# Cross-attention and FFN on one core: two more units take their probabilities through VectorE and memory

## The chip, the cores and the metric

The kernel runs on one core of a Trainium2 chip. The metric is the device time of one execution in microseconds; the median of three runs is given. Engines: TensorE (PE; its weight loads are PEld), VectorE (DVE), ScalarE (ACT), GpSimd (POOL), and SyncE (SP), whose queue issues nearly all DMAs, in the order in which they are written and each behind its own waits.

## The reference

```python
x = x + xattn(layernorm(x), ctx, mask, position_bias, ln_weight, w_q, w_k, w_v, w_out)
x = x + ffn(layernorm(x), ...)          # routed scales, sign(weight), bias

def xattn(hidden, kv, attention_mask, position_bias, ...):   # B=8, 128 x 128 tokens, D=512, H=32 heads of 128
    h_q, h_k, h_v = rmsnorm(hidden) @ w_q.T, kv @ w_k.T, kv @ w_v.T
    score = einsum('bqhd,bkhd->bhqk', h_q, h_k) + position_bias
    score = softmax(where(mask, score, -inf))
    score = where(mask, score, 0.0)
    attn = einsum('bhqk,bkhd->bqhd', score, h_v)
    return hidden + attn @ w_out.T
```

## The kernel before

**Stages.** Keys and values of all heads are computed first (to about 310 us of the span) and kept in memory. Then the queries of one pair of heads after another are computed, and between their matmuls the attention of earlier pairs and the output product run. The last stage, from about 755 us, is the FFN. Each large product is made of three matmuls in split precision (a high and a low part of each operand), and each group of 512 x 512 is made of seven such products, so that a group `n` has products 1 to 7, read by ScalarE or VectorE into `ring`.

**A unit** `j` is one head for four of the eight batches (`UNITS`, 64 of them; `j % 2` picks its buffers). Its steps are: `S` scores on TensorE (four 128 x 128 matmuls in two passes), `SC` bias added and row maximum on VectorE, `EXP` four exponentials on ScalarE, `N` scaling by the row sums on VectorE, a transposition, `PV` the context sums on TensorE (probabilities times values), `OH` and `OL` their high and low part on ScalarE and VectorE.

**Two ways to transpose.** A unit that is not in `BLOCKED` takes `T` and `PT`: TensorE transposes four 128 x 128 blocks into the PSUM bank `t` (line 1559), ScalarE copies the bank to `probs_t` (line 1038). A unit in `BLOCKED` takes `TZ`, `TS` and `TL`: ScalarE has written its exponentials to the bank `t` (`exps_of`), VectorE scales them there (line 1302) and transposes 32 x 32 blocks into `probs` (line 1307, `turn_probs`); SyncE issues four stores to `p_turned` in memory (line 762, `probs_store`), waits for them, and loads the blocks at their places to `probs_t` (line 768, `probs_load`). `PV` of such a unit waits for that load. Before, units 0 to 3 and 56 to 63 take the first way and units 4 to 55 the second.

**The order of the work is written out by hand** in `schedule()`: one list of steps, and each engine (SyncE's queue too) walks through those that are its own, in that order. There is no reordering: an instruction that waits holds all behind it on its engine. The units 0 to 3 stand in the branch `p == 0`; from unit 4 on, `aside(j, ...)` writes one unit: `PV` of `j - 2`, `S` and `EXP` of `j + 1`, load of the turned `j`, `normal(j + 1)`, and other work between. In the branch `p == 0` the groups are `first` = 33 and `n` = 34; `load` is the load of the query weights for the group after (`WL`, line 686), `sums` POOL's sums of them (`WS`, lines 855 to 860) and the first split (`WX`, on ScalarE line 971, on POOL line 867); `WOL` is the load of output weights (line 805), `BL` of a position bias (line 798), `KL` of keys (line 781).

**Semaphores that matter.** `d_pstore` and `d_pload` (one for each parity) count stores and loads of turned probabilities; `probs_load(j)` waits for the four stores of `j` and for `PV` of `j - 2`; `scores(j)` waits until `probs` of `j - 2` has been stored or transposed; `exponentials(j)` into the bank `t` wait until that of `j - 1` has been turned or copied.

Of the kernel before, what the change touches and what calls it, by code (L numbers as in the profile page):

```python
# [71 lines left out]
SPLIT = NH - 4  # L72
# [3 lines left out]

BLOCKED = range(4, 2 * SPLIT)


def bias_of(j):
# [9 lines left out]
def parts_of(step):  # L92
    kind, *index = step
    parts = PARTS_OF.get(kind, (kind,))

    if kind == "OUT" and index[0] == LAST - 1:
        parts = parts[:1]
    return [(part, *index) for part in parts]


def schedule():
# [93 lines left out]
    def product(n, i):  # L195
        return [("P", n, i), (READ[i], n)] + ([("SAVE", n, READ[i])] if n < NKV and READ[i] in RESULT else [])
# [47 lines left out]
    def biased(j):  # L244
        found = [("BM", j + 2)]
        if bias_of(j + 2) != bias_of(j + 3):
            found += [("BL", bias_of(j + 2) + 2)]
        return found

    def aside(j, early, middle, late, read_behind=()):  # L250
        found = [("PV", j - 2)] if j - 2 in BLOCKED else [("PV", 3)] if j == 4 else []
        found += [*read_behind, ("S", j + 1), ("EXP", j + 1), *biased(j)]
        return [*found, *early, ("TL", j), *normal(j + 1), *middle, *late]

    def last_aside(j, n, middle):

        six_five, c22 = product(n, 5), product(n, 7)
        found = [("PVH", j - 2), ("S", j + 1), ("EXP", j + 1), *biased(j), *six_five, ("OL", j - 2), *c22]
        if j == 7:

            found = [("PVH", j - 2), ("SP", j + 1), *six_five, ("SC", j + 1), ("EXP", j + 1), *biased(j), ("OL", j - 2), *c22]
        return [*found, ("TL", j), *normal(j + 1), *middle]

    def normal(j):
        return [("N", j), ("TZ", j), ("TS", j)] if j in BLOCKED else [("N", j)]

# [3 lines left out]
    def outs(p, *which):  # L270
        return [("OUT", p, b) for b in which]

    q = at[QUERIES[0]]
    for p in range(SPLIT // 2):
        j = 4 * p
        n = q + p + 2
        prod = {i: product(n, i) for i in SLOT}
        m = NPAIR + p + 2
        load, sums = [], []
        if n + 1 < len(GROUPS):  # L280
            load = [("WL", m + 1, 0), ("WL", m + 1, 1)]
            sums = [("WS", m + 1), ("WX", m + 1, 0)]
        if p == 0:

            first = q + 1
            steps += [*product(first, 7), *prod[1], ("N", 1), ("WX", m, 2), ("PV", 0), ("SMALL",)]
            steps += [("S", 2), *product(first, 3), ("T", 1), ("EXP", 2), ("BM", 3), ("BL", 3), *prod[6], ("N", 2), ("PV", 1)]
            steps += [("S", 3), *product(first, 4), *prod[2], ("WX", m, 3), ("T", 2), ("EXP", 3), ("BM", 4), *prod[5], ("N", 3),
                      ("PV", 2), ("WOL", 1), *load]
            steps += [*prod[7], ("S", 4), *prod[3], ("T", 3), ("EXP", 4), ("BM", 5), ("BL", 4), *prod[4],  # L290
                      *outs(0, 0), *normal(4), ("KL", 2), *sums, *outs(0, 1)]
            continue
        o = p - 1
        final = 2 * p + 2 == SPLIT


        if p == 1:
            steps += aside(j, outs(o, 2, 3) + prod[1], [("WX", m, 1)], [])
            steps += aside(j + 1, load + outs(o, 4, 5), [*prod[6], ("VV", p + 1), ("WX", m, 2), ("WX", m, 3)], [])
            steps += aside(j + 2, outs(o, 6) + prod[2], [*sums[:1], *outs(o, 7)], [("WO", p)])  # L300
            steps += last_aside(j + 3, n, [("WOL", p + 1), prod[3][0], ("KL", p + 2), *sums[1:]])
            continue
        steps += aside(j, product(n - 1, 4) + outs(o, 0), [*outs(o, 1), *prod[1], ("WX", m, 1)], [], read_behind=product(n - 1, 3)[1:])
        steps += aside(j + 1, load + outs(o, 2, 3), [*prod[6], ("VV", p + 1), ("WX", m, 2), ("WX", m, 3)], outs(o, 4))
        steps += aside(j + 2, outs(o, 5) + prod[2], [*outs(o, 6), *sums[:1]], outs(o, 7) + [("WO", p)])
        if final:
            steps += aside(j + 3, prod[5] + prod[7], [("WOL", p + 1), ("PV", j + 2), *prod[3], *prod[4], ("KL", p + 2), ("WO", p + 1)],
                           [*outs(p, 0, 1), ("PV", j + 3), ("VV", p + 2)])
        else:
            steps += last_aside(j + 3, n, [("WOL", p + 1), prod[3][0], ("KL", p + 2), *sums[1:]])  # L310
# [3 lines left out]
    j = 2 * SPLIT  # L314
# [11 lines left out]
    steps = [part for step in steps for part in parts_of(step)]  # L326
# [23 lines left out]

def xattn_ffn(nc, x, ctx_t, mask, pos_bias, ln_w, wq, wk, wv, wo, ffn_w, ffn_bias, gate_t, scales, out):
    steps = schedule()
    group_at = {group: n for n, group in enumerate(GROUPS)}

    def count(*kinds):
        found = [step for step in steps if step[0] in kinds]
        assert len(set(found)) == len(found)
        return {step: n + 1 for n, step in enumerate(found)}
# [20 lines left out]
    def nth_own(j):  # L379

        return len([unit for unit in BLOCKED if unit <= j and unit % 2 == j % 2])

# [11 lines left out]
    for kind in ("T", "PT"):  # L394
        assert [step[1] for step in count(kind)] == [j for j in range(len(UNITS)) if j not in BLOCKED]
    unit_at = {unit: j for j, unit in enumerate(UNITS)}

    with ExitStack() as ctx:
# [154 lines left out]
        def exps_of(j):  # L553

            return t_bank[:].rearrange("p (b k) -> p b k", b=HALF) if j in BLOCKED else probs[:, j % 2]

# [110 lines left out]
        def _(sp):  # L667
# [89 lines left out]
            def probs_store(j):  # L757
                sp.wait_ge(v_turn, nth_turn["TZ", j])
                if j - 2 in BLOCKED:
                    sp.wait_ge(d_pload[j % 2], 16 * nth_own(j - 2))  # L760
# [948 lines left out]
```

## Time and profile before

| | |
|---|---|
| median of 3 runs | 800.81 us (800.28 to 801.17) |
| the profiled execution's own time | 800.34 us |
| its span | 798.5 us |
| PE busy | 793.7 us (99%) |
| DVE busy | 636.6 us (80%) |
| ACT busy | 359.2 us (45%) |
| POOL busy | 296.7 us (37%) |
| DMA | 145.53 MB, mean 182 GB/s |

The profile is of one execution. Matmuls are pipelined: a matmul's duration is longer than the distance to the next one's start, and it is the distance that fills the time. In a timeline, `x4` means that four instructions are merged into one row.

### The profile page before, as it was taken

How to read it: one execution, taken by the hardware profiler on the slowest of the kernel's cores; microseconds unless marked ns; L12 is line 12 of the kernel's file. 1: busy time of each engine (PE TensorE's matmuls, PEld its weight loads, DVE VectorE, ACT ScalarE, POOL GpSimd, SP SyncE). 2: the span in 40 equal slices, each digit the busy share in tenths (PEclk: the TensorE clock that was granted, in tenths of full speed). 3: DMA queues.
4: the chain of work that ended last, by engine and by line, in shares of the span. 5: the costliest groups of instructions: out<-in, count | busy, mean ns of one | idle time of the engine just before them, and what ended most of it. 6: DMA issues, size and time to landing. Idle time of an engine off the chain costs nothing.

```text
span 798.5 us, 12698 instructions
## 1 busy us (share of the span) xinstructions
PE 793.7 (99%) x4090; PEld 674.9 (85%) x4090; DVE 636.6 (80%) x1066; ACT 359.2 (45%) x949; POOL 296.7 (37%) x279
## 2 busy tenths in 40 slices
PE   9999999999999999999999999999999999999998
PEld 7888888888888888888888888888888888888886
DVE  6877878886893596888888788888888888877775
ACT  6633432432341253545444444444444444447683
POOL 3113021020111032736535544644564454435136
PEclk9999999999999999999999999999999999999999
DMA  8354774584466658627755766575566657553002
GB/s 301 146 196 174 224 247 138 175 266 161 154 191 205 206 166 275 207 65 226 236 163 163 239 191 205 163 240 171 175 210 202 204 157 240 162 196 141 1 1 106
DMA packets 103216, 145.53 MB, mean 182 GB/s; under 512 B 9944, under 2 KB 74584, under 8 KB 97648
## 3 DMA queue, kind: packets, MB, share of 16 engines
q1 hardware_dynamic: 102720, 144.33, 55.5%
q8 instruction: 34, 0.56, 0.3%
q10 hardware_dynamic: 432, 0.39, 0.2%
q14 instruction: 30, 0.25, 0.1%
HBM read 93.31 MB, written 51.38 MB: 181 GB/s over the span
## 4 chain that ended last, share of the span: by engine, by line
PE 98%; DMA 1%; DVE 0%; issue 0%; ACT 0%; SPq 0%; DVEq 0%
PE out L1455 11%; PE out L1457 11%; PE out L1456 11%; PE proj L1457 10%; PE proj L1455 10%; PE proj L1456 10%; PE o L1575 7%; PE s L1549 7%; PE s L1456 4%; PE s L1455 4%; PE s L1457 4%; PE proj L1651 1%; PE t L1603 1%; PE proj L1652 1%; PE t L1559 1%; DMA early<-in_ctx_t 1%
## 5 line engine op out<-in xcount | busy, mean ns | idle before, releaser
L1030 ACT ACTIVATE t<-probs,neg_max 128x128 f32<-128x128 f32 x208 | 74.2, 357 | 112.2 <-DVE neg_max L1295 112.1
L855 POOL TENSOR_TENSOR w_stage<-w_stage 128x256 f32<-128x256 f32 x30 | 24.7, 824 | 264.8 <-DMA w_stage<-in_wk 236.4
L867 POOL TENSOR_TENSOR w_lo<-w_stage,w_hi 128x512 fp32r<-128x512 f32 (+1 forms) x52 | 59.2, 1148 | 134.7 <-ACT w_hi L971 134.7
L1455 PE MATMUL out<-wo_hi,o_hi 128*128 128x512 f32 x224 | 90.6, 405 | 0.1
L1457 PE MATMUL out<-wo_lo,o_hi 128*128 128x512 f32 x224 | 87.8, 392 | 0.0
L1456 PE MATMUL out<-wo_hi,o_lo 128*128 128x512 f32 x224 | 87.4, 390 | 0.0
L1455 PE MATMUL proj<-x_hi,w_hi 128*128 128x512 f32 x210 | 85.0, 405 | 0.0
L1457 PE MATMUL proj<-x_lo,w_hi 128*128 128x512 f32 x210 | 82.4, 392 | 0.0
L1456 PE MATMUL proj<-x_hi,w_lo 128*128 128x512 f32 x210 | 81.8, 390 | 0.0
L879 POOL TENSOR_TENSOR bias_mask<-bias_raw,mask_neg 128x512 f32<-128x512 f32 x64 | 75.7, 1184 | 13.8 <-DVE probs L1292 13.6
L1332 DVE TENSOR_TENSOR acc<-out,acc 128x512 f32<-128x512 f32 x100 | 66.6, 675 | 7.1 <-PE out L1457 7.0
L971 ACT ACTIVATE w_hi<-w_stage 128x512 fp32r<-128x512 f32 (+1 forms) x113 | 61.7, 565 | 18.3 <-POOL w_stage L857 6.6
L1048 ACT ACTIVATE o_hi<-o 128x512 fp32r<-128x512 f32 x60 | 35.4, 590 | 43.5 <-PE o L1575 43.3
L1314 DVE TENSOR_TENSOR o_lo<-o,o_hi 128x512 fp32r<-128x512 f32 x60 | 41.2, 686 | 16.3 <-ACT o_hi L1048 16.3
L1292 DVE TENSOR_TENSOR probs<-s,bias_mask 128x512 f32<-128x512 f32 x64 | 43.7, 682 | 9.5 <-PE s L1549 9.5
L1457 PEld LDWEIGHTS out<-wo_lo,o_hi 128*128 128x128 f32 x224 | 42.1, 188 | 9.3
L888 POOL TENSOR_TENSOR wo_lo<-wo_raw,wo_hi 128x1024 fp32r<-128x1024 f32 x14 | 33.6, 2403 | 42.0 <-ACT wo_hi L1056 42.0
L1160 DVE TENSOR_TENSOR w_lo<-w_stage,w_hi 128x512 fp32r<-128x512 f32 (+1 forms) x61 | 44.6, 732 | 5.7 <-ACT w_hi L971 5.2
L1455 PEld LDWEIGHTS out<-wo_hi,o_hi 128*128 128x128 f32 x224 | 42.2, 188 | 8.2 <-issue 0.5
L1456 PEld LDWEIGHTS out<-wo_hi,o_lo 128*128 128x128 f32 x224 | 42.3, 189 | 7.9
L1457 PEld LDWEIGHTS proj<-x_lo,w_hi 128*128 128x128 f32 x210 | 39.4, 188 | 8.6
L1456 PEld LDWEIGHTS proj<-x_hi,w_lo 128*128 128x128 f32 x210 | 39.7, 189 | 7.4
(362 smaller groups left out, 2100.9 us busy)
## 6 DMA issues: line engine op xcount, KB each, us to landing
k_spill<-ring SPq DMA_DIRECT2D x64, 256.0 KB, 3.4
v_spill<-ring SPq DMA_DIRECT2D x64, 256.0 KB, 2.5
p_turned<-probs SPq DMA_DIRECT2D x208, 64.0 KB, 1.8
probs_t<-p_turned SPq DMA_DIRECT2D x52, 256.0 KB, 4.3
big_stage<-in_wv SPq DMA_DIRECT2D x8, 1024.0 KB, 7.9
w_stage<-in_wq SPq DMA_DIRECT2D x32, 256.0 KB, 3.3
k_first<-k_spill SPq DMA_DIRECT2D x8, 1024.0 KB, 6.0
v_first<-v_spill SPq DMA_DIRECT2D x8, 1024.0 KB, 5.1
```

The source lines that it names most:

```text
L867: pool.tensor_tensor(lo, staged(m, part), hi.bitcast(F32), ALU.subtract).then_inc(g_wlo, 1)
L879: pool.tensor_tensor(bias_mask[:, j % 2], bias_raw[:, i % 2][:, None, :].to_broadcast([P, HALF, P]), mask_neg[:, halves[half], :], ALU.add ...
L971: act.activation(hi, staged(m, part), ACT.Copy).then_inc(a_whi, 1)
L1030: last = act.activation(exps_of(j)[:, b], probs[:, j % 2, b, :], ACT.Exp, bias=neg_max[:, col:col + 1], accum_out=row_sum[:, col:col + 1])
L1160: dve.tensor_tensor(lo, staged(m, part), hi.bitcast(F32), ALU.subtract).then_inc(v_wlo, 1)
L1292: dve.tensor_tensor(probs[:, j % 2], s_bank[j % 2][:].rearrange("p (b k) -> p b k", b=HALF), bias_mask[:, j % 2], ALU.add).then_inc(v_scor ...
L1332: dve.tensor_tensor(acc[:, b, :], bank_tensor[:], acc[:, b, :], ALU.add).then_inc(v_acc, 1)
L1455: pe.matmul(to[:], left_hi, right_hi, start=first and n == 0, stop=False, skip_group_check=True)
L1456: pe.matmul(to[:], left_lo, right_hi, start=False, stop=False, skip_group_check=True)
L1457: last = pe.matmul(to[:], left_hi, right_lo, start=False, stop=n == len(pairs) - 1, skip_group_check=True)
L1549: last = pe.matmul(to[:, b * P:(b + 1) * P], queries[:, b * P:(b + 1) * P], keys, start=True, stop=True)
L1575: last = pe.matmul(to[:, b * P:(b + 1) * P], v_tiles[p % 2][:, half * HALF + b, i * P:(i + 1) * P], moving, start=True, stop=True)
```

## The change

`BLOCKED` begins with unit 2 in place of unit 4, so that units 2 and 3 are turned by VectorE and memory as well; `TensorE`'s transposes and ScalarE's copies of these two go. The context sums of unit 2 move from behind product 5 of group 34 to behind its product 7, ahead of the scores of unit 4. In `aside` only the two cases for the first units are written in another way: `PV` of unit 3 still opens `aside(4)`.

```diff
-BLOCKED = range(4, 2 * SPLIT)
+BLOCKED = range(2, 2 * SPLIT)
...
     def aside(j, early, middle, late, read_behind=()):
-        found = [("PV", j - 2)] if j - 2 in BLOCKED else [("PV", 3)] if j == 4 else []
+        found = {4: [("PV", 3)], 5: []}.get(j, [("PV", j - 2)])
...
             steps += [*product(first, 7), *prod[1], ("N", 1), ("WX", m, 2), ("PV", 0), ("SMALL",)]
-            steps += [("S", 2), *product(first, 3), ("T", 1), ("EXP", 2), ("BM", 3), ("BL", 3), *prod[6], ("N", 2), ("PV", 1)]
-            steps += [("S", 3), *product(first, 4), *prod[2], ("WX", m, 3), ("T", 2), ("EXP", 3), ("BM", 4), *prod[5], ("N", 3),
-                      ("PV", 2), ("WOL", 1), *load]
-            steps += [*prod[7], ("S", 4), *prod[3], ("T", 3), ("EXP", 4), ("BM", 5), ("BL", 4), *prod[4],
+            steps += [("S", 2), *product(first, 3), ("T", 1), ("EXP", 2), ("BM", 3), ("BL", 3), *prod[6], *normal(2), ("PV", 1)]
+            steps += [("S", 3), *product(first, 4), *prod[2], ("WX", m, 3), ("TL", 2), ("EXP", 3), ("BM", 4), *prod[5], *normal(3),
+                      ("WOL", 1), *load]
+            steps += [*prod[7], ("PV", 2), ("S", 4), *prod[3], ("TL", 3), ("EXP", 4), ("BM", 5), ("BL", 4), *prod[4],
                       *outs(0, 0), *normal(4), ("KL", 2), *sums, *outs(0, 1)]
```

`normal(j)` is `N`, `TZ`, `TS` for a unit in `BLOCKED` and `N` alone for another.

## Rows read from the trace of the kernel before

**Rows 1.** The page: the chain that ended last, share of the span by engine.
```profile
PE 98%; DMA 1%; DVE 0%; issue 0%; ACT 0%; SPq 0%; DVEq 0%
```

**Rows 2.** Waits of TensorE: waiter, releaser, total us, times, longest us.
```profile
PE s L1532 <- DVE ring L1124: 1.1, 1, 1.1
```

**Rows 3.** Windows by engine: length, busy times, PEclk, DMA share, GB/s.
```profile
343.00:345.00 2.00, 2.00 (x12) 1.69 (x11) 1.97 (x4) 1.36 (x3) 0.87 (x1) 1.00 0.00 0
```

**Rows 4.** Timeline of TensorE: start us, length us, instruction.
```profile
343.21 0.39 PE L1457 MATMUL proj<-x_lo,w_hi 128*128 128x512 f32 x1
343.44 0.60 PE L1559 MATMUL t<-ident,probs 128*128 128x128 f32 x4
343.79 0.48 PE L1455 MATMUL proj<-x_hi,w_hi 128*128 128x512 f32 x1
344.11 0.40 PE L1456 MATMUL proj<-x_hi,w_lo 128*128 128x512 f32 x1
...
354.54 1.06 PE L1575 MATMUL o<-probs_t,v_first 128*128 128x128 f32 x8
...
359.10 0.39 PE L1455 MATMUL proj<-x_hi,w_hi 128*128 128x512 f32 x1
```

**Rows 5.** Timeline of ScalarE, the first exponential of unit 3.
```profile
345.13 0.40 ACT L1030 ACTIVATE probs<-probs,neg_max 128x128 f32<-128x128 f32 x1
```

**Rows 6.** Timeline of VectorE, units 2 and 3, and the turn of unit 4.
```profile
342.10 0.69 DVE L1302 TENSOR_TENSOR probs<-probs,inv_sum 128x512 f32<-128x512 f32 x1
...
344.02 0.69 DVE L1295 TENSOR_REDUCE neg_max<-probs 128x4 f32<-128x512 f32 x1
...
346.80 0.18 DVE L1300 RECIPROCAL inv_sum<-row_sum 128x4 f32<-128x4 f32 x1 [0.29 <-ACT probs L1030]
...
355.21 0.70 DVE L1302 TENSOR_TENSOR t<-t,inv_sum 128x512 f32<-128x512 f32 x1
355.94 0.72 DVE L1307 STREAM_TRANSPOSE probs<-t 128x512 f32<-128x512 f32 x1
```

**Rows 7.** Timeline of SyncE's queue: start us, issue us, DMA.
```profile
337.93 0.42 SPq L805 DMA_DIRECT2D wo_raw<-in_wo  x1
338.46 1.21 SPq L686 DMA_DIRECT2D w_stage<-in_wq  x2
...
356.69 1.79 SPq L762 DMA_DIRECT2D p_turned<-probs  x4
...
359.81 0.34 SPq L768 DMA_DIRECT2D probs_t<-p_turned  x1
```

**Rows 8.** Landings: all turned loads, those at 377.4 and 366.5, query weights.
```profile
DMA to landing us min/median/max: 2.6/4.3/6.6
...
DMA to landing us min/median/max: 2.7/2.7/2.7
...
DMA to landing us min/median/max: 4.5/4.5/4.5
...
w_stage<-in_wq SPq DMA_DIRECT2D x2, 256.0 KB, 4.1
```

**Rows 9.** Instructions of line 1575, context sums: ns min/median/max, first and last start.
```profile
L1575 PEld LDWEIGHTS o<-probs_t,v_first x256: 186/192/192, 333.6 to 749.0; 128*128 128x128 f32 x128
L1575 PE MATMUL o<-probs_t,v_first x256: 270/275/377, 333.8 to 749.1; 128*128 128x128 f32 x128
```

**Rows 10.** Timeline of POOL: query sums, and the low part behind them.
```profile
345.27 1.23 POOL L855 TENSOR_TENSOR w_stage<-w_stage 128x256 f32<-128x256 f32 x1
...
347.97 1.19 POOL L860 TENSOR_TENSOR w_stage<-w_stage 128x256 f32<-128x256 f32 x1
...
353.31 0.73 POOL L867 TENSOR_TENSOR w_lo<-w_stage,w_hi 128x256 fp32r<-128x256 f32 x1 [4.15 <-ACT w_hi L971]
```

**Rows 11.** The first matmuls: line 1532's instructions, and TensorE's timeline.
```profile
L1532 PE MATMUL s<-ring x22: 274/421/583, 1.1 to 5.1; 128*128 128x128 f32 x22
...
1.05 4.36 PE L1532 MATMUL s<-ring 128*128 128x128 f32 x22 [1.05 <-DVE ring L1124]
```

## The prediction

> **What bounds the kernel now.** I read the page's busy shares and its chain of work first, then the waits, then the timeline of each engine where the change acts. TensorE is busy 99% of the span and carries 98% of the chain that ended last [rows 1]. The longest wait in TensorE's list is 1.1 us, for the first tile of the whole kernel [rows 2]. So the kernel is TensorE's own instruction stream. An instruction taken out of that stream is a gain of its pace; a wait put into it is a loss of its whole length, because nothing later in the stream is slack that could give it back. Around the change TensorE is busy 2.00 us of 2.00, while the DMA share is 0.00 [rows 3]: the bytes that the change adds meet an empty path, and only latency counts.
>
> **Part 1, what leaves TensorE.** The timeline of TensorE gives the price of a turned unit [rows 4]. The last matmul of product 2 starts at 343.21, the four transposes at 343.44, product 5 at 343.79 and its second matmul at 344.11. Without the transposes the second matmul would start two paces of 0.23 after 343.21, at 343.67. So a unit's transposes cost 0.44 us (0.35 for the four, 0.09 for the longer step behind a group of 128-column matmuls). Units 2 and 3: 2 x 0.44 = 0.88 us. The move of the context sums of unit 2 to stand directly before the scores of unit 4 removes one such longer step, 0.09. Together 0.97 us, all on the path. ScalarE's copies of the two units also go; ScalarE is not on the path, and the gain there is nothing.
>
> **Part 2, what unit 2 now needs, step by step.** Nothing changes before VectorE scales the probabilities of unit 2, at 342.10 [rows 6]. The exponentials ahead of it now write to PSUM, but four of them keep their pace of 0.39 us. The scaling of a PSUM tile starts 0.73 before its 32x32 transpose, which lasts 0.72 (355.21 and 355.94, unit 4 of before) [rows 6]. So the turn of unit 2 starts at 342.83 and ends at 343.55. SyncE's queue then issues four stores and, when they have landed, the load: for unit 4 the stores start at 356.69, 0.03 after the turn ended, and the load at 359.81, 3.12 later [rows 7]. There too the path was empty when the stores began. So unit 2: stores at 343.58, load at 346.70. From issue to landing such a load takes 2.6 to 6.6 us, median 4.3; the load at 377.4 took 2.7 and the load at 366.45, right behind two weight loads, 4.5 [rows 8]. The load of unit 2 has nothing beside it, so I take 2.65: landed at 349.35. Another 0.2 goes between landing and the first matmul: the weight loads of line 1575 start at 333.6 and its matmuls at 333.8 [rows 9]: context sums at 349.55.
>
> When would TensorE be there? Product 5 starts at 343.79 less 0.35; it and product 7 take 6 paces of 0.23 each, so TensorE is at the moved sums at about 346.20. It waits 349.55 - 346.20 = **3.35 us**. In the kernel before, the blocked units have the cover that this one lacks: unit 4 is turned at 356.66, and its sums come some 9 us later, with a whole unit between. Unit 2 is turned at 343.55 and its sums come 2.65 us later, less than the stores alone take. The move behind product 7 buys 1.38 us and is not enough. For bounds: landing at 2.6 gives a wait of 3.30; landing at the median 4.3 gives 5.0; at 6.6 it gives 7.3, for which something large would have to be beside it.
>
> **Part 3, unit 3.** VectorE is 0.76 us later behind the turn of unit 2 (0.12 for the longer step, 0.64 for the transpose). The row maximum of unit 3 then starts at 344.78 instead of 344.02 and ends at 345.47. Its exponentials run from 345.51 and not from 345.13 (where they stood behind the copy that goes), and 1.68 later, at 347.19 and not 346.80, VectorE takes the reciprocal [rows 5, 6]. Scaling and turn follow as for unit 2. Turn at 348.33 to 349.05, stores from 349.08. Behind them in SyncE's queue stand, moved from 337.93 and 338.46, the output weights (512 KB) and two query-weight loads (256 KB each) [rows 7], which now issue from about 350.9 to 352.5. Only then comes the load of unit 3, at 352.6. It lies behind 1 MB, as the one at 366.45 did behind half of that; I take its 4.5 us: landed at 357.1, matmul at 357.3. TensorE comes to the sums of unit 3 at 354.54 [rows 4] + 3.35 - 0.97 = 356.92. **A further 0.35 us**; with 2.7 us for the load none, with 6.6 us 2.5.
>
> **Part 4, what was moved past in the queues.** The query weights land some 4.1 us behind their issue [rows 8], at about 356.1 instead of 343. POOL's four sums took 3.9 us from 345.27 and its low part of the first split 0.73 [rows 10]: now done at 360.8 at the latest. ScalarE's high part of that split waits for the landing too, with only the next context copy behind it, whose sums are no earlier than 357.3. TensorE wants that split at 359.10 [rows 4] + 2.7 = 361.8: hidden, by 1 us. Were TensorE not held by unit 2, it would want it at 358.1, and 1 to 2.7 us would show. The output weights aren't wanted until after 370. The next bias, behind the load of unit 3, is two units early. VectorE has 1.44 us more of transposes; the wait of TensorE hides them, since it starts on nothing while unit 2 is away. Cost nothing.
>
> **The sum.** -0.97 + 3.35 + 0.35 = +2.73 us. The profiled execution took 800.34 us (span 798.5 and 1.84 around it), so its like would take 803.1. The three timed runs have the median 800.81, 0.47 above the profiled one; the changed kernel's median should lie there as well, at **803.5 us**, 0.34% slower. A measurement of this kernel can tell about 0.2% from no change, 1.6 us.
>
> **The rivals.**
> A, the clock follows the stall. The granted clock is 1.00 in all rows, but the first matmuls of the kernel run slower: a median of 421 ns against 275 of the same shape later [rows 9, 11]. That is the lower of the two levels (1.2 against 2.4 GHz), with TensorE idle before it. If 3.35 us of idling brings that level back, the 22 matmuls that spread over 4.36 us there [rows 11] (0.20 each, against 0.09 for each of the four transposes of 128 columns at 343.44 [rows 4]) say what it costs: half the time so run, about 2.2 us. Sum: 805.7. For it: no stall like this exists in the trace, so nothing excludes it. Against it: it is a single gap.
> The Trainium skill, "TensorE: Matmul & The Clock Gate", section "Why this matters for your kernels", speaks for this rival: it tells to avoid idle gaps between bursts of matmuls of about the length forecast here, for throughput drops behind them. No row of this trace shows a gap that long.
> B, the transfers are slower than their quiet price, or unit 3's load suffers as the worst of its kind: 1 to 2.5 us more, 804.5 to 806.
> C, the other side (not slower): the turned probabilities of unit 2 are there in time. It needs the way through memory to be 3.35 us shorter, 2.45 from turn to landing against 5.8 here, or unit 2's softmax to run that much earlier, by VectorE's queue being less full than in this execution. Then only part 1 is left, 799.8, more if the query weights of part 4 come late. It decides once the wait is under 0.97 us. No row is near: even the shortest landing of all, 2.6, takes longer by itself than this 2.45.
> D, the change doesn't do what it says in full: only part of the wait shows, because TensorE runs late at this place anyhow. Between 0.97 and 2.5 us of wait the result is within 0.2%: about 801.6.
>
> **How the numbers follow.** Forecast 0.62, A 0.10, B 0.13, C 0.05, D 0.10. The forecast's own range is 802.7 to 804.3: 0.35 of part 3 gone and the medians 0.4 apart, or 0.4 more for each of the two loads. The range over the cases takes in A, B and the upper half microsecond of D: 802.2 to 806.0. The whole gain of part 1 is 0.12%, so C is within 0.2% too, unless part 1 is undersized by as much again: faster by over 0.2% gets 0.02, within 0.2% (D and the rest of C) 0.13, slower 0.85.
>
> **What would show it.** A gap of TensorE of 3.3 us ahead of the sums of unit 2 at about 346.2, released by the DMA of the turned probabilities; the turn of unit 2 ending at 343.5 and SyncE's load at 346.7; a small gap or none ahead of the sums of unit 3; no gap ahead of product 1 of the next group; everything after 360 shifted by 2.7 us and otherwise equal; and the chain of waits naming DMA with some 3 us more. Wrong would be: no gap at 346 (C), matmul paces of over 0.3 us behind the gap (A), landings over 4 us for unit 2 (B), or a second gap at 361.8, which would say that the moved weight loads were not covered.

## The result

The changed kernel takes 804.52 us (median of six runs, 802.66 to 806.12), the kernel before, beside it, 800.71 (six runs, 800.12 to 801.52). The ratio is 1.0049, with a 95% interval of 1.0039 to 1.0060: slower by 0.5%. The profiled execution took 805.68 us with a span of 803.9, against 800.34 and 798.5 before.

| | before | after |
|---|---|---|
| median | 800.71 us | 804.52 us |
| spread of the runs | 1.4 us | 3.5 us |
| span of the profiled execution | 798.5 us | 803.9 us |
| longest wait of TensorE | 1.1 us | 4.5 us |

The page of after, its busy line and its chain of work. The chain answers to [rows 1]: TensorE's share fell from 98% to 94%, while its busy time rose by 1.1 us although it has 8 instructions fewer. The 4 points are not a price: the chain now comes to the sums of unit 2 through its turn, and so it follows VectorE and ScalarE from 322 to 343 us, a stretch in which TensorE was busy as before.

```profile
PE 794.8 (99%) x4082; PEld 676.0 (84%) x4082; DVE 636.4 (79%) x1068; ACT 358.7 (45%) x947; POOL 296.1 (37%) x279
...
PE 94%; DVE 2%; issue 1%; DMA 1%; POOL 1%; ACT 1%; SPq 0%; DVEq 0%; POOLq 0%
```

TensorE's waits in after (waiter, releaser, total us, times, longest us) answer to [rows 2]. One line is new, and it is four times as long as the longest before.

```profile
PE o L1575 <- DMA probs_t<-p_turned: 4.5, 1, 4.5
PE s L1532 <- DVE ring L1124: 1.1, 1, 1.1
```

TensorE's timeline of after at the place of [rows 4]: the last matmul of product 7, then the sums of unit 2, the scores of unit 4, and the first matmul of product 3.

```profile
346.27 0.39 PE L1457 MATMUL proj<-x_lo,w_hi 128*128 128x512 f32 x1
351.15 2.08 PE L1575 MATMUL o<-probs_t,v_first 128*128 128x128 f32 x8 [4.50 <-DMA probs_t<-p_turned]
353.02 1.55 PE L1549 MATMUL s<-k_second,ring 128*128 128x128 f32 x8
354.33 0.49 PE L1455 MATMUL proj<-x_hi,w_hi 128*128 128x512 f32 x1
```

From the start of the last matmul, 346.27, the next could begin one pace of 0.23 later, at 346.50; it began at 351.15. That is a wait of 4.65 us from start to start (the 4.50 in brackets counts from the modelled end). Then the sums take 1.87 us and the scores 1.31, where two such groups took 0.90 and 0.81 from 354.54 to 356.25 before: 1.5 us more. The windows show a lower granted clock just there: 0.62 on average, in its middle 0.50 (the lower level, 1.2 GHz), and 1.00 after.

```profile
347.00:351.00 4.00, 0.00 (x0) 0.00 (x0) 2.55 (x6) 0.18 (x2) 0.00 (x0) 0.95 0.32 88
351.00:355.00 4.00, 3.85 (x19) 3.75 (x20) 1.08 (x2) 0.60 (x1) 0.00 (x0) 0.62 0.89 256
355.00:359.00 4.00, 4.00 (x19) 3.27 (x18) 2.59 (x5) 1.96 (x9) 2.30 (x4) 1.00 0.39 133
...
350.00:351.00 1.00, 0.00 (x0) 0.00 (x0) 0.00 (x0) 0.00 (x0) 0.00 (x0) 0.82 0.82 279
352.00:353.00 1.00, 1.00 (x6) 1.00 (x6) 0.00 (x0) 0.00 (x0) 0.00 (x0) 0.50 0.80 172
```

The way of unit 2 through memory, on the chain that ended last (start us, length us, what), and SyncE's queue of after, which answers to [rows 7]:

```profile
344.98 3.44 DMA p_turned<-probs
...
348.43 2.68 DMA probs_t<-p_turned
...
351.15 1.01 PE o L1575 x3
```

```profile
343.63 1.79 SPq L762 DMA_DIRECT2D p_turned<-probs  x4
348.43 0.34 SPq L768 DMA_DIRECT2D probs_t<-p_turned  x1
349.10 1.76 SPq L762 DMA_DIRECT2D p_turned<-probs  x4
350.91 0.45 SPq L805 DMA_DIRECT2D wo_raw<-in_wo  x1
351.46 1.21 SPq L686 DMA_DIRECT2D w_stage<-in_wq  x2
352.76 0.55 SPq L768 DMA_DIRECT2D probs_t<-p_turned  x1
```

The stores begin at 343.63, the load at 348.43: 4.80 us, not 3.12 as for unit 4 before, because the last of the four stores took 3.4 us to land; why it did no run shows. The load itself needed 2.7. Everything later is shifted and otherwise as before: the scores of unit 5 start at 360.82 against 355.44, 5.38 later, and the span is 5.4 longer. So all of the loss lies in these few microseconds: 0.36 by which this execution was behind before the change begins (scores of unit 3 at 340.13 against 339.77), -0.97 of removed work, 4.65 of wait; the 1.36 left over go with the clock.

### The profile page after: what moved, and what is told of

Read it like the earlier page. It is cut to its first block, busy times and chain, and to the rows that moved or that the text cites. A ratio compares the mean times of both kernels' runs of the same rounds, so it can differ in the third digit from the quotient of the medians.

```text
span 803.9 us, 12694 instructions
## 1 busy us (share of the span) xinstructions
PE 794.8 (99%) x4082; PEld 676.0 (84%) x4082; DVE 636.4 (79%) x1068; ACT 358.7 (45%) x947; POOL 296.1 (37%) x279
## 4 chain that ended last, share of the span: by engine, by line
PE 94%; DVE 2%; issue 1%; DMA 1%; POOL 1%; ACT 1%; SPq 0%; DVEq 0%; POOLq 0%
PE out L1455 11%; PE out L1457 11%; PE out L1456 11%; PE proj L1457 10%; PE proj L1455 10%; PE proj L1456 10%; PE o L1575 7%; PE s L1549 7%; PE s L1456 4%; PE s L1457 4%; PE s L1455 4%; PE t L1603 1%; PE s L1532 1%; DVE w_lo L1160 1%; POOL acc L929 0%
## 5 line engine op out<-in xcount | busy, mean ns | idle before, releaser
L1030 ACT ACTIVATE t<-probs,neg_max 128x128 f32<-128x128 f32 x216 | 77.1, 357 | 115.7 <-DVE neg_max L1295 115.7
```

The costliest lines, as they stand in the source:

```text
L1030: last = act.activation(exps_of(j)[:, b], probs[:, j % 2, b, :], ACT.Exp, bias=neg_max[:, col:col + 1], accum_out=row_sum[:, col:col + 1])
```

## The experiments

Two readings stand against each other. **W**: the loss is the wait of the sums of unit 2 and the clock behind it. **Q**: the moved loads, the fuller queues and VectorE's transposes cost as well. In what follows the "offset" of a trace is how much later than before its scores of unit 3 start, ahead of anything that the change touches; it lies between -0.1 and 0.9 us. It is not made by the edits: in every trace it is there to within 0.1 us already 13 us earlier, in the scores that start at 326.95 before and at 327.29 in after.

### The changed kernel again

No edit.

> The changed kernel, once more, to see how much its wait and its clock vary from execution to execution. In the trace of after TensorE waits 4.5 us for the turned probabilities of unit 2, because the last of the four stores took 3.4 us to land where those of unit 4 took 1.6 to 1.8, and the granted clock is 0.50 from 351 to 354. Theory W (the wait, with the clock behind it): the wait is between 3.3 and 4.7 us here, the clock falls to 0.50 for 2 to 4 us behind it or not at all, and the span is that of before + wait - 1.0, and 1.5 us more where the clock fell; median 803.5 to 805. Theory Q (the moved weight loads and the fuller queues cost as well): the span is longer than this sum by 1 us or more, with a second gap of TensorE near 360.

Measured: 803.74 us (803.43 to 804.34, five runs), ratio 1.0041 (1.0028 to 1.0054), span 801.6.

```profile
348.70 1.16 PE L1575 MATMUL o<-probs_t,v_first 128*128 128x128 f32 x8 [2.50 <-DMA probs_t<-p_turned]
349.70 1.75 PE L1549 MATMUL s<-k_second,ring 128*128 128x128 f32 x8
351.09 0.78 PE L1455 MATMUL proj<-x_hi,w_hi 128*128 128x512 f32 x1
```

```profile
351.00:355.00 4.00, 4.00 (x16) 3.24 (x15) 2.29 (x4) 1.65 (x8) 0.00 (x0) 0.71 0.89 276
```

TensorE's timeline and a window of this run: the wait is 2.65 from start to start, below the range expected, since here the stores took 3.11 to the load and all landed at once. The clock fell all the same, this time behind the sums, which still have their full pace: it is the scores and product 3 that are slow. The sum 798.5 - 0.08 (offset) - 0.97 + 2.65 is 800.1, and the span is 801.6: 1.5 us for the clock. There is no second gap of TensorE. W holds for this trace; its lower bound for the wait was 0.65 us too high. The other four executions, which have no trace, took 803.47 to 804.34 with a mean clock of 0.999 to 1.00: what they did not lose to the clock they must have lost to a longer wait, or elsewhere. Which, no run shows.

### The wait filled with work

```diff
+            def fill(j):
+                to = take(o_bank)
+                for _ in range(14):
+                    pe.matmul(to[:], x_hi[:, 0, 0, 0:P], x_hi[:, 0, 0], start=True, stop=True)
...
-            steps += [*prod[7], ("PV", 2), ("S", 4), *prod[3],
+            steps += [*prod[7], ("FILL", 2), ("PV", 2), ("S", 4), *prod[3],
```

> The changed kernel with 14 matmuls of 512 columns (14 x 0.23 = 3.2 us) on tiles that are at hand, written to the bank of the context sums just before the sums of unit 2 overwrite it. The matmuls fill most of the wait, nothing else changes. Theory W with the clock as a cost of its own: the granted clock stays at 1.00, the sums and scores behind the wait take 0.89 and 0.80 us in place of 1.87 and 1.31, and the span is 1.5 us shorter than that of the changed kernel with its clock fallen, although TensorE does 3.2 us more work; median about 803. Rival (the clock falls for another reason, or the slow sums come from the memory traffic of that moment): sums and scores stay slow, and the median stays near 804.5. If the matmuls were not hidden in the wait, it would be 807 or more.

Measured: 802.91 us (802.67 to 805.68, five runs), ratio 1.0038 (1.0026 to 1.0050), span 802.4. Timeline of TensorE and windows:

```profile
346.98 3.33 PE L1583 MATMUL o<-x_hi 128*128 128x512 f32 x14
...
350.99 1.16 PE L1575 MATMUL o<-probs_t,v_first 128*128 128x128 f32 x8 [0.67 <-DMA probs_t<-p_turned]
351.98 1.06 PE L1549 MATMUL s<-k_second,ring 128*128 128x128 f32 x8
352.79 0.49 PE L1455 MATMUL proj<-x_hi,w_hi 128*128 128x512 f32 x1
```

```profile
351.00:355.00 4.00, 4.00 (x26) 3.60 (x27) 2.15 (x4) 0.74 (x2) 0.00 (x0) 1.00 0.74 208
```

The clock stays at 1.00; sums and scores take 0.99 and 0.81. From 346.98, where TensorE would have been free, to the sums 4.01 us pass, almost as long as in after, and 798.5 + 0.86 (offset) - 0.97 + 4.01 is 802.4, the span to the tenth: nothing is left over for a clock. So 3.3 us more of work cost nothing in this execution. For the clock there is also the mean of each execution: none of the five here is at 0.998 or below, of the changed kernel's eleven (six of the result and five of the repeat) five are, but of the five of the repeat only one. That points to the idling, and the runs below, by the length of their gaps, do so more strongly. The times alone do not show it: the intervals of this run and the one before overlap.

### Unit 2 without its wait

The context sums of unit 2 read a tile of values in place of the turned probabilities (so the output of these heads is not the reference's); turn, stores and load stay.

```diff
-                if j in BLOCKED:
+                if j in BLOCKED and j != 2:
                     pe.wait_ge(d_pload[j % 2], 16 * nth_own(j))
-                else:
+                elif j != 2:
                     pe.wait_ge(a_pt, nth_t["T", j])
...
+                    if j == 2:
+                        moving = v_tiles[0][:, b, 0:P]
```

> The changed kernel, but the context sums of unit 2 read another tile (values that are there since before) and so don't wait for the turned probabilities; the output is not the reference's for these heads. Turn, stores and load of unit 2 all stay, in their places. Theory W: without this wait all that is left is the gain of TensorE, -1.0 us, and at most 1 us each of wait for unit 3 (whose stores, behind the moved loads, land at about 357 where TensorE now comes at 353.6) and for the moved query weights (done by 360, wanted at 358). So a gap of up to 3.5 us ahead of the sums of unit 3, and a median of 800 to 803. Theory Q: the gaps remain further on, and the median stays at 803.5 or more.

Measured: 805.58 us (802.85 to 806.16, five runs), ratio 1.0056 (1.0044 to 1.0068). Without the wait the kernel is no faster, rather slower. W had expected 800 to 803 and is missed; by time and place it is what Q expected, 803.5 or more with the gaps further on. TensorE's timeline and SyncE's queue:

```profile
346.44 1.05 PE L1577 MATMUL o<-v_first 128*128 128x128 f32 x8
...
357.44 2.08 PE L1577 MATMUL o<-probs_t,v_first 128*128 128x128 f32 x8 [3.37 <-DMA probs_t<-p_turned]
```

```profile
352.72 0.55 SPq L768 DMA_DIRECT2D probs_t<-p_turned  x1
```

The sums of unit 2 go at 346.44, at once. Then TensorE waits 3.4 us for unit 3, whose load is issued at 352.72 behind three weight loads and lands 4.7 us later, at 357.4. W's expectation had named this gap ("up to 3.5 us ahead of the sums of unit 3") and yet allowed for no fall of the clock behind it; it fell here too and for longer (0.50 from 357 to 363 us): 798.5 + 0.3 - 0.97 + 3.52 is 801.4, the span 804.4. So the wait of unit 2 hides another one of nearly the same size, in the same span of time. W is right for the changed kernel as it stands, and the moved loads and fuller queues of Q cost as soon as that wait is gone.

### The weight loads back in their place

```diff
-            steps += [("S", 2), ..., ("BM", 3), ("BL", 3), *prod[6], *normal(2), ("PV", 1)]
+            steps += [("S", 2), ..., ("BM", 3), ("BL", 3), ("WOL", 1), *load, *prod[6], *normal(2), ("PV", 1)]
...
-                      ("WOL", 1), *load]
+                      ]
```

> The changed kernel, with the output weights' load and the two query weight loads put back ahead of the stores of unit 2 in SyncE's queue (where they stood before the change, at about 338). Theory W: they were hidden in after, so nothing moves for them; but the load of unit 3 now has a quiet path, 2.7 us in place of 4.3, which is hidden too. Median as the changed kernel's, 803.5 to 805, unit 2's wait the same 3.3 to 4.7. Theory Q: 1 us or more is won back, 803 or less, without a shorter wait of unit 2.

Measured: 803.75 us (802.67 to 808.78, seven runs), ratio 1.0047 (1.0030 to 1.0063); the changed kernel beside it 803.74. In the trace TensorE waits 2.5 us for unit 2, less than the 3.3 expected, and for nothing else around it. The load of unit 3 takes 2.7 us. As W says, the moved loads cost nothing while the wait of unit 2 stands ahead of them. The slowest execution, 808.78 with a mean clock of 0.995, has no trace.

### The sums at their old place

```diff
-                    ..., *prod[5], *normal(3), ("WOL", 1), *load]
-            steps += [*prod[7], ("PV", 2), ("S", 4), *prod[3],
+                    ..., *prod[5], *normal(3), ("PV", 2), ("WOL", 1), *load]
+            steps += [*prod[7], ("S", 4), *prod[3],
```

> The changed kernel with the context sums of unit 2 at their old place, behind product 5 instead of product 7 of the same group (six matmuls, 1.38 us, earlier). Theory W: TensorE comes 1.4 us earlier and leaves at the same moment, so the wait is longer by 1.4 us (4.7 to 6.1), and product 7 comes behind it: the span grows by 1.4 us and by 0.1 for one more step behind 128-column matmuls, median about 805.5 to 806.5, and the clock falls in all executions (it fell in four of six with the shorter wait). Rival (the move is worth nothing, as the wait is made by something that moves along with TensorE): the same time as the changed kernel.

Measured: 805.11 us (804.87 to 805.49, four runs), ratio 1.0057 (1.0043 to 1.0070). The wait is 4.0 us where the first repeat had 2.5, with the same 3.14 us from stores to load. So the move behind product 7 was worth about its six matmuls of cover, 1.4 us, as forecast. The wait itself is below the range expected (4.7 to 6.1), which started from the 4.5 of after, and the time is 0.4 us under the expectation. The mean clock is 0.998 in all four executions.

### The sums later still

```diff
-            steps += [*prod[7], ("PV", 2), ("S", 4), *prod[3],
+            steps += [*prod[7], ("S", 4), *prod[3], ("PV", 2),
```

> The changed kernel with the context sums of unit 2 moved on, behind the scores of unit 4 and product 3. They now have 2.2 us more of work ahead of them. Theory W: the wait shrinks by 2.2 us, to 1.1 to 2.5, and with so short a wait the clock stays up; median 0.9 to 1.5 us above before's less 1, so 801 to 802.5, within 0.2% of before. Theory Q: nothing changes but the place of the loss, 803.5 or more.

Measured: 804.67 us (803.76 to 805.66, four runs), ratio 1.0051 (1.0037 to 1.0065), against W's expectation of 801 to 802.5: missed, and in Q's range, 803.5 or more. TensorE's timeline:

```profile
349.21 1.16 PE L1575 MATMUL o<-probs_t,v_first 128*128 128x128 f32 x8 [0.26 <-DMA probs_t<-p_turned]
...
352.21 0.48 PE L1455 MATMUL out<-wo_hi,o_hi 128*128 128x512 f32 x1 [0.45 <-issue]
...
358.05 2.08 PE L1575 MATMUL o<-probs_t,v_first 128*128 128x128 f32 x8 [2.84 <-DMA probs_t<-p_turned]
```

The wait of unit 2 shrank to 0.3 us, and what it gave back went to unit 3 (2.8 us, and the fall of the clock with it) and to the first output product (0.45). For this one the trace names no releaser; it needs the low part of the sums that have just moved towards it, and VectorE ends that at 352.11, 0.10 ahead of it (the two runs below with such a gap show the same 0.10). The mean clock is 0.998 in all four. It is what the run without the wait showed, with the true data.

### Each unit alone

Unit 2 alone (`BLOCKED = [2, *range(4, 2 * SPLIT)]`, `T` of unit 3 again, and its wait on VectorE's turns counts to that of unit 2):

> Unit 2 alone is turned by VectorE and memory (with its sums behind product 7), unit 3 by TensorE as before. Theory W: the whole loss is unit 2's, so this is the changed kernel with 0.44 us more for the transposes of unit 3: wait 3.3 to 4.7, median 804 to 805.5. Rival (unit 3's longer way through the queue behind 1 MB of weights is a part of the loss): 803.5 or less.

Measured: 803.54 us (802.82 to 804.68, four runs), ratio 1.0038 (1.0024 to 1.0052). That is 0.5 us under W's expectation and at the edge of its rival's (803.5 or less), so the time does not decide. The trace does: the whole wait is there with unit 2 alone. TensorE's timeline and a window:

```profile
349.31 1.16 PE L1575 MATMUL o<-probs_t,v_first 128*128 128x128 f32 x8 [2.72 <-DMA probs_t<-p_turned]
350.31 1.06 PE L1549 MATMUL s<-k_second,ring 128*128 128x128 f32 x8
```

```profile
351.00:355.00 4.00, 4.00 (x23) 3.35 (x22) 2.96 (x5) 1.80 (x8) 1.97 (x3) 1.00 0.29 96
```

In this execution the wait was as long as in the first repeat, and the clock stayed up. The sum 798.5 + 0.29 - 0.53 + 2.87 is 801.1, and the span is 801.1. This pair measures the two terms apart: wait and removed work account for all of the span when the clock holds, and 1.5 us more is there when it falls.

Unit 3 alone, with the weight loads ahead of its stores (`BLOCKED = range(3, 2 * SPLIT)`):

```diff
+            steps += [..., ("T", 2), ("EXP", 3), ("BM", 4), *prod[5], ("WOL", 1), *load, *normal(3), ("PV", 2)]
```

> Unit 3 alone is turned by VectorE and memory, unit 2 by TensorE as before, and the output and query weights stay ahead of the stores of unit 3. Theory W: the turn of unit 3 ends at about 348.6, its stores have landed at 351.8 to 353.4 and its load 2.7 later, at 354.5 to 356; TensorE is there at 354.1. So a wait of 0.5 to 2 us against a gain of 0.44: median 800.7 to 802.5, no clock fall. Rival (a unit's way through memory hides as soon as nothing else stands in the queue): no wait, 800.3.

Measured: 801.21 us (800.83 to 804.39, eleven runs), ratio 1.0011 (1.0002 to 1.0020). No wait for the probabilities of unit 3: its load starts at 353.02 and the sums at 355.55. What TensorE waits for is VectorE. Its timeline, then VectorE's:

```profile
351.07 0.50 PE L1455 MATMUL proj<-x_hi,w_hi 128*128 128x512 f32 x1 [0.39 <-DVE ring L1144]
```

```profile
349.12 0.72 DVE L1307 STREAM_TRANSPOSE probs<-t 128x512 f32<-128x512 f32 x1
...
350.34 0.67 DVE L1144 TENSOR_TENSOR ring<-proj,ring 128x512 f32<-128x512 f32 x1
```

The addition that frees the bank of product 7 stands behind the turn and comes at 350.34; product 4 wants that bank at 350.5. From start to start this gap is 0.55 us. So the time was in W's range, and the mechanism was Q's, not W's. Two executions, 802.47 and 804.39, were slower with the clock up; they have no trace.

### Neither unit waits

As the third run, with both units' sums reading other data (the output of these heads is not the reference's): `j != 2` becomes `j > 3` and `j not in (2, 3)`, `if j == 2` becomes `if j in (2, 3)`.

> The changed kernel, but the context sums of unit 2 and of unit 3 read another tile and wait for no turned probabilities (the output is not the reference's for these heads); turns, stores and loads stay. The run before it, with unit 2 alone so treated, had its loss not gone but moved: TensorE waited 3.4 us for unit 3 and its clock fell. Theory W2 (two waits of nearly the same end, the one of unit 3 behind that of unit 2 and the loads; nothing else costs): no wait for probabilities; what is left is the gain of 0.97, and at most 1 to 2.7 us ahead of product 1 of the next group, wanted at 358.1 less what the split of the moved query weights takes (done at 359 to 360.3). Span 797.5 to 800, median 799.7 to 802, clock 1.00. Rival (VectorE's two more transposes or the queues cost on their own): 803 or more without any wait for probabilities.

Measured: 802.18 us (801.20 to 804.60, seven runs), ratio 1.0026 (1.0014 to 1.0039). TensorE's timeline and POOL's:

```profile
360.42 0.47 PE L1455 MATMUL proj<-x_hi,w_hi 128*128 128x512 f32 x1 [1.90 <-POOL w_lo L867]
```

```profile
356.65 0.74 POOL L855 TENSOR_TENSOR w_stage<-w_stage 128x256 f32<-128x256 f32 x1 [10.70 <-DMA w_stage<-in_wq]
...
358.86 0.73 POOL L860 TENSOR_TENSOR w_stage<-w_stage 128x256 f32<-128x256 f32 x1
359.54 0.73 POOL L867 TENSOR_TENSOR w_lo<-w_stage,w_hi 128x256 fp32r<-128x256 f32 x1
```

A third layer: with both waits for probabilities gone TensorE waits for the split of the query weights, whose loads the change moved from 338 to 351. The prediction had it ("1 to 2.7 us would show"). The clock fell behind this wait too (0.50 from 361 to 364 us in the trace), which the expectation had excluded, and the median is 0.2 us above its range. Three of the seven executions have a mean clock of 0.998 and took 803.4 to 804.6, the other four 801.2 to 802.2. Without a trace of one of the four this difference can't be split into wait and clock.

### Cover for all three

Sums of unit 2 behind product 3, weight loads ahead of the stores:

> The kernel with the sums of unit 2 behind product 3, and the output and query weights' loads back ahead of the stores of unit 2. In the run with the later sums alone TensorE waited 0.3 us for unit 2 and then 2.8 for unit 3, whose load was issued at 352.7, behind 1 MB of weights, and landed 5 us later. Theory W2 (the load of unit 3 is slow because of the weights ahead of it): it is issued at 352.3, lands in 2.7, at 355.0; wait for unit 3 of 0 to 0.5 us, clock 1.00, median 800 to 801.5. Rival (the landing has nothing to do with the weights): the wait stays 2 us or more, 803.5 or more.

Measured: 802.12 us (801.11 to 804.11, eleven runs), ratio 1.0019 (1.0011 to 1.0028). SyncE's queue and TensorE's timeline:

```profile
352.46 0.34 SPq L767 DMA_DIRECT2D probs_t<-p_turned  x1
```

```profile
352.53 0.47 PE L1454 MATMUL out<-wo_hi,o_hi 128*128 128x512 f32 x1 [0.89 <-issue]
355.36 1.05 PE L1574 MATMUL o<-probs_t,v_first 128*128 128x128 f32 x8
```

The load of unit 3 is issued 0.2 us earlier than with the later sums alone and lands in 2.7 us instead of 5.3; its wait is gone. So the weights ahead of it made it slow: with them there, such a load took 4.3 to 5.3 us in seven traces. What is left is 0.3 us for unit 2 and 0.9 ahead of the output product. The traced execution is the fastest of the eleven (801.11), so the others waited longer for something that no trace shows; the median is 0.6 us above the expectation.

Both sums later, those of unit 3 behind two output products:

```diff
+        if j == 4:
+            early = [*early[:2], ("PV", 3), *early[2:]]
+            found = []
```

> As the run beside it, and the sums of unit 3 stand two output products and the scores of unit 5 later (3.6 us of cover more). Both units now have cover. Theory W2: no wait for unit 3, at most 0.3 to 1.9 us for unit 2; the gain of 0.9 us shows when the stores of unit 2 land quickly: median 799.8 to 801. That would equal or beat the kernel before by at most 0.9 us. Rival (VectorE's queue, with the softmax of unit 5 now ahead of the low parts of unit 3, makes other waits): a wait of TensorE for VectorE, 801 to 803.

Measured: 801.39 us (800.87 to 802.02, eleven runs), ratio 1.0005 (0.9996 to 1.0014): not to be told from before, and a little above the expectation. The two small waits stay (0.40 and 0.82).

With the scores of unit 5 moved ahead of the first output product, to fill the second (`aside(4)` keeps only their bias and maximum, `SC`):

```diff
-                      *outs(0, 0), *normal(4),
+                      ("SP", 5), *outs(0, 0), *normal(4),
```

> As the kernel with both sums later, and TensorE's scores of unit 5 stand before the first output product instead of behind the second. In the run before TensorE waited 0.4 us for unit 2's load and then 0.8 us ahead of the first output product, for the low part of the context of unit 2, which VectorE makes 1.4 us behind the sums. Theory W2: the scores (0.8 us) fill that second wait, so the span falls by 0.8 us to 798.3, and the median from 801.4 to 800.6 or less: the gain of TensorE (0.9) and the wait that is left (0.4 and up, by how fast the stores of unit 2 land) cancel, and the kernel is as fast as before, 800.2 to 800.8. Rival (the second wait has another cause than the low part): it stays, 801.4.

Measured: 801.73 us (800.88 to 802.46, eleven runs), ratio 1.0013 (1.0003 to 1.0022). The wait ahead of the first output product is gone, and another has come:

```profile
349.24 1.16 PE L1577 MATMUL o<-probs_t,v_first 128*128 128x128 f32 x8 [0.40 <-DMA probs_t<-p_turned]
...
357.58 0.47 PE L1457 MATMUL out<-wo_hi,o_hi 128*128 128x512 f32 x1 [0.59 <-DVE acc L1326]
```

Of the eight tenths in one place, six are lost again to VectorE's addition in another, and a step 0.2 us longer stays behind the scores: nothing is won. The expectation of 800.2 to 800.8 was missed by this. No version with unit 2 or 3 through memory was faster than the kernel before.

## Why the prediction was right, and where not

**The bound** was right: in the traces whose clock held, each wait of TensorE appeared in the span in full, and every other engine's work stayed hidden or showed only where TensorE waited for it.

**Part 1**, -0.97 us: no run measures it by itself, but it closes the sum to 0.1 us in the two traces whose clock held (the filled wait, and unit 2 alone with its -0.53).

**Part 2**, 3.35 us, was the main term and had the right place, releaser and steps. The turn ended at 343.61 (forecast 343.55), the stores began at 343.63 (343.58). The length was 4.65 in the profiled execution and 2.65 to 2.87 in the quieter ones. Three sizes differ. The distance from stores to load is 3.1 to 3.2 in nine of the twelve traces that have a turned unit 2, and 4.35 to 4.8 in the other three, which the single row of unit 4 could not show. The first matmul starts 0.04 us behind the landing, not 0.2; the trace puts the first weight load at the same moment. And the stores begin earlier by TensorE's own time: 3.4 to 3.7 us behind the scores of unit 3 in all twelve, against 3.81 in the forecast (343.58 less 339.77). That the stores of after come within 0.05 us of the forecast is luck, for its TensorE was 0.36 late by then and its VectorE only 0.05. VectorE's place beside TensorE differs from execution to execution, and the one row of before had it late: there the scaling of unit 2 starts 2.33 us behind those scores, and 2.04 in the run that turns unit 3 alone and leaves unit 2 as it was. VectorE's timelines of the first repeat and of that run:

```profile
342.32 0.72 DVE L1307 STREAM_TRANSPOSE probs<-t 128x512 f32<-128x512 f32 x1
```

```profile
342.42 0.69 DVE L1302 TENSOR_TENSOR probs<-probs,inv_sum 128x512 f32<-128x512 f32 x1
```

In the first repeat this is 0.44 of the 0.7 us by which its wait was shorter than the forecast; the load, 2.49 us in place of 2.65, and the step behind it give the most of the rest.

**Part 3**, 0.35 us for unit 3: none in after, since the longer wait for unit 2 covered it. Its working was right to some tenths, the load issued at 352.76 (forecast 352.6) and landed in 4.3 (4.5). What the prediction did not draw from it is that this wait stands just behind the first, and takes over when the first is removed; the run without unit 2's wait and the one with the later sums show it.

**Part 4** was right: hidden in after by the wait, and 1.9 us where the wait was taken away. VectorE's 1.44 us, put at nothing with the wait of TensorE named as cover, are hidden in after, and 0.39 us where unit 3 alone is turned (0.55 from start to start). The last version, where both units have some cover, shows 0.59 for VectorE in another place.

**Rival A**, the clock, had a chance of 0.10 and a price of 2.2 us. It came true in both traced executions of the changed kernel, and the sum of the forecast has no term for it: that is where its account is short. The mean clock is 0.998 in four of the six and 0.997 in one of the five of the repeat. By what is left over of the two traced spans the fall costs 1.4 to 1.5 us. The price of 2.2 was worked out from the first matmuls of the kernel, and there the granted clock of before reads 1.00 (from 0 to 6 us), so that these rows do not show the lower level; what does is the windows of after. The argument against A, that it is a single gap, was no reason. With the clock up, the quiet wait of 2.65 us would give a span of 800.1 and a time near 802 (an estimate), and none of the eleven executions was that fast: the fastest took 802.66. In the profiled execution the slow stores (2 us) and the clock (1.4 us) stand above it, in the first trace of the repeat the clock (1.5 us); for the other nine, six of them with the clock up, no trace says what does. So the forecast of 803.5 came near by luck: of two errors that partly cancel, a wait set 0.7 us too long for a quiet execution, and a clock and a straggler left out. How often each of the two comes is open.
The Trainium skill, "TensorE: Matmul & The Clock Gate", section "Why this matters for your kernels", tells to avoid idle gaps between bursts of matmuls, for throughput drops behind them. The traces agree that the clock falls behind such a gap, but no length divides them here: 1.9 us in one execution and 2.5 us in two were followed by a fall, and 2.7 us in another was not.

**Rivals B, C and D**: B's slow transfer came, in a quarter of the traces, with the stores; the load of unit 2, in which its sign looked for it (over 4 us), landed in 2.5 to 2.7 us and once in 3.4. C and D did not come in any trace of the changed kernel.

**The time** of 804.52 is above the forecast's own range, 802.7 to 804.3, and within the whole range, by the ranges of A and B.

## What to carry to other kernels

Before a step is sent through memory on the ground that the bound engine gets rid of work, count the time from the last instruction that makes the data to the first that needs it: in the first repeat 5.7 us were needed (343.04 to 348.70) and 3.0 were there (to 346.04), against a gain of 0.44 us a unit. A wait on the bound engine can hide others behind it, so a repair that removes only the first may win nothing; look for what would be late next, and mend them together. And price a gap of TensorE higher than its length, since the clock may fall behind it. Take the wait from more than one execution, too: its two ends are made by two engines, and here they stood up to 0.4 us apart from the one row that the forecast had.

## What the runs showed of the hardware

- **The clock behind a gap.** Gaps of TensorE of 2.5, 2.5, 2.8, 3.4, 4.0 and 4.5 us were followed by a granted clock of 0.50 (the lower level, 1.2 GHz), one of 1.9 us too, and one of 2.7 us was not. The fall can come when TensorE has been at work again for more than a microsecond: in the first repeat the sums at 348.70 had their full pace and the scores at 349.70 had not. By what the sums leave over it cost 1.4 to 1.8 us each time, and 3.0 in the run where it stayed down longest. Over all executions, traced or not, a mean of 0.998 or below goes roughly with the length of the gap in the run's trace: the sums at their old place and the later sums (4.0 and 2.8 us) 8 of 8, the run without unit 2's wait (3.4) 4 of 5, the weight loads back in their place (2.5) 4 of 7, the changed kernel (4.5 and 2.5) 5 of 11, neither unit waiting (1.9) 3 of 7, unit 2 alone (2.7) 1 of 4, and the five versions with gaps under 1 us 1 of 49. What else decides is open.
- **A slow store now and then.** The same four stores of 64 KB, on a path that is nearly idle, took 3.1 to 3.2 us from the first issue to the load in nine of twelve traces, and 4.8, 4.65 and 4.35 in three; those of unit 3 took 4.07 once. The cause is open. In after it is the last store alone that is late (3.4 us to land, the others 1.6 to 2.0).
- **A load behind others.** The load of turned probabilities of unit 2 or 3 took 4.3 to 5.3 us in the seven traces where 1 MB of weights was issued just ahead of it. In the 17 cases without them it took 2.5 to 2.7, and 3.4 and 3.8 once each.
